# Two of four batches' gates, choices, places and scatters moved from behind the attention into its later pairs

## The chip, the cores and the metric

The kernel runs on one core of a Trainium2 chip. The metric is the device time in microseconds (us) of one execution. Five instruction queues run beside one another and meet only at semaphores: PE (TensorE, matrix products, with PEld for its weight loads), DVE (VectorE), ACT (ScalarE), POOL (GpSimd) and SP (SyncE, which here only issues DMAs).

## The reference

```
x = x + attention(layernorm(x))     # x: 4 batches x 512 tokens x 128; 16 heads of 8, causal, rotary
x = x + ffn(layernorm(x))           # first mixture of experts
x = x + scan_block(layernorm(x))    # convolution, linear recurrence over 512 steps, gate
x = x + ffn(layernorm(x))           # second, same weights

def ffn(x):                         # 2048 tokens, 8 experts, hidden width 512
    scores = sigmoid(x @ Wg.T + bg + bias)
    top_scores, top_idx = top_k(scores, 2)
    # every token: two experts, each gelu(x @ W1[e].T + b1[e]) @ W2[e].T + b2[e], weighted by its score
    # plus one shared expert that every token passes: gelu(x @ Ws1.T + bs1) @ Ws2.T + bs2
```

## The kernel before, in words

**Attention** works through 32 pairs of heads, eight pairs to a batch, so batch b is in pairs 8b to 8b+7. In pair n, PE makes the plain scores of pair n+2 in three units (`scores`, S), DVE takes their row maxima (`row_max`, line 1894, then `split_max`, line 1903), PE makes the turned scores of pair n with the maximum folded in (`scores_T`, T, also three units, line 1360), ACT takes their exponential (`exps`, line 960) and PE weighs the values with them (`weigh_values`, line 1385). Every second pair ACT copies the weighed sums (line 965), PE folds them (line 1397) and DVE divides (lines 1911, 1912). All S and T units, and the few units of the next batch's projections and of the last batch's output projection ("at", "wo"), take turns in three PSUM slots in an order written out by hand (`ring_order`): a unit waits until the unit three turns ahead of it has been read. Lists such as `XN_IN` and `STATS_IN` say behind which pair a side job stands. From pair 17 on ACT and DVE also split the expert weights into high and low halves (lines 1015 and 1953) behind each pair. POOL rotates queries and keys of the next batch (`rope`, lines 766 to 780) and is idle from the end of the last rotation to the end of the attention.

**First feed-forward stage**, behind the attention. For each batch: statistics (`norm_stats`, line 1853), inverse root on POOL (line 729), normalised tokens (`norm_apply`, line 1867), turned on PE (`tokens_T`) and copied by ACT, gate products (`gates`, line 1540) and a sigmoid on ACT, then on DVE `choose` (lines 2059 to 2072: the two best of eight), PE's counts of earlier tokens (`ranks`, line 1552), and `place` (lines 2084 to 2104: the row of each token in its experts' lists). POOL splits the tokens into two halves (`split_rows`) and sends them to those rows in DRAM with eight indirect DMAs a batch (`scatter`, line 879). Some of these wait for named PE units (`BEHIND`), so that they go out spread. Beside this runs the shared expert of each batch: `shared_up` on PE, `shared_hidden` on ACT (lines 1129 and 1140) into one buffer `hid`, `shared_low` on DVE (line 2132), `shared_down` on PE (line 1583), `shared_back` on ACT (line 1149) and `own_outputs` on PE. Since there is one `hid`, a batch's `shared_hidden` waits for the `shared_low` of the batch before it. `map_tiles` (lines 2109 to 2125) turns the filled lists into 39 tiles of 128 rows. PSUM goes round eight banks in a second order written out by hand (`bank_order`). PE fills some waits with products that nobody reads (`stay_awake`, line 1506).

**Tiles**: SP loads each tile's expert weights and rows, PE multiplies (lines 1632, 1646, 1647). SP asks for the first rows when all scatters have landed and the last `shared_low` is done. Then come the scan block, and a second feed-forward stage with the same functions called with r = 1.

The norms are counted: `norm_stats` number n writes `mean[:, n % 8]`, POOL's root of it waits for `var_ready` n+1. In DVE's queue, the order behind the loop of pairs is:

```
for b in range(B - 1): norm_stats(x_all[:, b], core_link, X_SCALE)
for b in range(B - 1): tokens(b)
...
divide(QUADS - 1); tokens_split(0); tokens_split(1); choose(0, 0); attention_post(B - 1); ...
place(0, 0); tokens(3); experts_of(1); experts_of(2); experts_of(3); shared_low(0, 0); ...
```

Of the kernel before, what the change touches and what calls it, by code (L numbers as in the profile page):

```python
# [11 lines left out]
I32 = mybir.dt.int32  # L12
# [33 lines left out]
STATS_IN = {0: 2, 8: 3}  # L46
TOPS_TO = [0, 0, 0, 1, 2, 3, 5, 6, 8, 8, 10, 11, 13, 14] + [16] * (PAIRS - 13)
# [28 lines left out]
EARLY_FILLS = 2 * (PAIRS - FILLS_FROM) - len(SLOTS_IN)  # L76
FFN_LINKS = 7
# [11 lines left out]
def ring_order():  # L89
# [4 lines left out]
    for n in range(PAIRS):  # L94
# [71 lines left out]
def bank_order():  # L166
# [15 lines left out]
    def of_choice(b):  # L182
        return [("gr", 0, b), ("rt", 0, b)]

    order += [("gx", 0, 0), ("gx", 0, 1), ("gg", 0, 0), ("gx", 0, 2), ("gg", 0, 1), ("gg", 0, 2)] + of_choice(0)
    order += of_shared(0, 0) + of_choice(1) + [("gx", 0, 3), ("gg", 0, 3)] + of_choice(2) + of_shared(0, 1) + of_choice(3)
    for b in range(B):
        order += [("sd", 0, b)]
        if b + 2 < B:
            order += of_shared(0, b + 2)  # L190
        order += [("ba", 0, b)]
# [24 lines left out]
RINGS = {"all": (1, 3, 5, 7, 6, 0, 2, 4), "y": (0, 1), "wide": (2, 3, 4), "rest": (5, 6, 7)}  # L216
# [36 lines left out]
def hybrid_block_kernel(nc, x_in, wqkv_in, wo_in, bo_in, w1_in, b1_in, w2_in, b2_in, wg_in, gate_rows_in,  # L253
# [3 lines left out]
    with ExitStack() as ctx:  # L257
# [82 lines left out]
        route = sb("route", [P, TT, X])  # L340
# [55 lines left out]
        ownT = heads_arena[:, 2304:2304 + L]  # L396
        wt = part(arena, 0, [WT, WROW], F16)
# [22 lines left out]
        qk_words = qk_sb[:].rearrange("p t d -> p (t d)")  # L420
        xg = part(qk_words, 0, [XG, ROW], F16)
# [69 lines left out]
        idx_ready = sem("idx_ready")  # L491
        scattered = [sem(f"scattered{b}") for b in range(B)]
        map_ready = sem("map_ready")
        first_in = [sem(f"first_in{e}") for e in range(X)]
# [48 lines left out]
        def x16T_of(r, b):  # L543
            return x16T4[:, b] if r == 0 else x16T[:, b % 2]
# [10 lines left out]
        def xrow_of(r, b):  # L555
            return xrow4[:, b] if r == 0 else xrow[:, b % 2]

        def xrow_words_of(r, b):
            return xrow4_words[:, b] if r == 0 else xrow_words[:, b % 2]
# [32 lines left out]
        def _(sp):  # L592
# [33 lines left out]
            def fill(r, i, start, rows):  # L626
                of = grids[:, FILL_AT + 2 * i:FILL_AT + 2 * i + ROW // 2].bitcast(I32)
                sp.dma_start(rows_dram[r].ap()[start:start + rows, :].rearrange("(n p) d -> p n d", p=P),
                             of.unsqueeze(1).broadcast_to([P, rows // P, ROW // 2])).then_inc(zeroed, 16)
# [96 lines left out]
        def _(pool):  # L726
# [13 lines left out]
            nc.gpsimd.memset(route[:], 1.0)  # L740
# [58 lines left out]
            def take_last(e):  # L799

                pool.wait_ge(first_in[e], 32)
                raw = w1_raw[0:D - 1, e, :]
                nc.gpsimd.tensor_tensor(raw, raw, last_w1[0:D - 1, e * F:(e + 1) * F], ALU.subtract).then_inc(less_last, 1)

# [5 lines left out]
            for e in range(E // 2, E):  # L810
                take_last(e)
            pool.wait_ge(tops_found, 1)
# [3 lines left out]
            rope(3)  # L816

            norms = [B]
# [28 lines left out]
            def set_constants(rows):  # L847

                nc.gpsimd.memset(rows[:, :, :, D - 1], X_SCALE)
                link(nc.gpsimd.memset(rows[:, :, :, 2 * D - 1], 0.0))  # L850

            def split_rows(r, b):

                g = r * B + b
                pool.wait_ge(xf_ready, TT * (g + 1))
                if r == 0:
                    pool.wait_ge(pv_made, PAIRS - 1)
                elif b >= 2:
                    pool.wait_ge(scattered[b - 2], 16 * 2 * TT * 2)
                if g == 0:  # L860
                    set_constants(xrow4)
                high, low = (xrow_of(r, b)[:, :, k * D:(k + 1) * D - 1] for k in range(2))
                tokens = xf_of(r, b)[:, :, 0:D - 1]
                link(nc.gpsimd.tensor_copy(high, tokens))
                nc.gpsimd.tensor_tensor(low, tokens, high, ALU.subtract).then_inc(rows_ready, 1)

            def scatter(r, b):
                g = r * B + b
                pool.wait_ge(idx_ready, g + 1)
                if (r, b) == (1, B - 1):  # L870
                    pool.wait_ge(last_rows_ready, 1)
                else:
# [1547 lines left out]
```

## Time and profile before

| what | value |
|---|---|
| time of three runs | 555.2, 558.01 and 566.67 us, median 558.01 us |
| the profiled execution | 557.48 us, its span from first to last instruction 555.5 us |
| busy share of the span | PE 85%, DVE 77%, ACT 60%, PEld 56%, POOL 49% |
| mean granted TensorE clock | 0.952 of full speed |

The span is what the trace shows; the time of an execution has some us around it. The busy shares are means over very different stages, so the rows that matter are those of the later pairs and of the stage behind them.

### The profile page before, as it was taken

The numbers are of one execution on the slowest core, as the hardware profiler recorded it, in microseconds if no ns is written. First come the engines' busy times: TensorE is split into PE (matmuls) and PEld (weight loads), VectorE is DVE, ScalarE is ACT, GpSimd is POOL, SyncE is SP. The second block draws the span as 40 slices with busy tenths as digits, with TensorE's granted clock in tenths as the row PEclk, the third lists the DMA queues.
The fourth block names the chain that finished last, engine by engine and source line by source line (L and its number), as shares of the span: only waits on it lengthen the run. The fifth ranks groups of instructions, "written<-read, shape, count | busy, mean of one in ns | idle before, by whom it ended". The sixth has DMA issues, their size and how long they took to land.

```text
span 555.5 us, 14159 instructions
## 1 busy us (share of the span) xinstructions
PE 473.2 (85%) x4943; PEld 312.0 (56%) x4943; DVE 426.1 (77%) x1154; ACT 334.7 (60%) x509; POOL 270.8 (49%) x263
## 2 busy tenths in 40 slices
PE   7899988989999968789999898679999995998930
PEld 2436555655665645435579895124455653887930
DVE  5658689778899869777279985798899772888836
ACT  1337556666777773356479984246666861887830
POOL 5418597006400005687328766473275771566650
PEclk9979989999999999979899999979999998999985
DMA  4745796342531463111468691999010014796826
GB/s 130 187 150 169 210 227 156 103 127 81 145 98 32 119 190 106 35 44 49 133 198 260 206 301 54 247 194 170 3 38 20 31 53 126 221 286 197 265 66 200
DMA packets 88186, 78.16 MB, mean 141 GB/s; under 512 B 9917, under 2 KB 72790, under 8 KB 88118
## 3 DMA queue, kind: packets, MB, share of 16 engines
q1 hardware_dynamic: 76208, 57.81, 39.5%
q10 hardware_dynamic: 7366, 10.07, 5.9%
q0 software_dynamic: 4544, 9.38, 4.9%
q8 instruction: 41, 0.67, 0.5%
q14 instruction: 27, 0.22, 0.1%
HBM read 39.92 MB, written 30.88 MB: 127 GB/s over the span
## 4 chain that ended last, share of the span: by engine, by line
PE 31%; DVE 9%; issue 4%; DMA 3%; ACT 2%; SPq 1%; POOL 1%; POOLq 0%; DVEq 0%; ACTq 0%
PE ps L1632 9%; PE ps L1646 6%; PE ps L1647 3%; PE ps L1506 3%; PE ps L1583 2%; DMA arena<-y_dram 2%; PE ps L1622 2%; SPq L712 1%; DVE x_all L2188 1%; PE ps L1718 1%; PE ps L1561 1%; PE ps L1708 1%; DVE arena L2132 1%; DMA y_dram<-arena,goes_to 1%; PE ps L1596 1%
## 5 line engine op out<-in xcount | busy, mean ns | idle before, releaser
L1894 DVE TENSOR_REDUCE max_words<-ps 128x2 f32<-128x256 f32 (+3 forms) x128 | 98.6, 819 | 28.4 <-PE ps L1334 28.2
L888 POOL DMA_INDIRECT y_dram<-arena,goes_to x78 | 86.4, 1108 | 64.7 <-DVE goes_to L2147 35.0
L960 ACT ACTIVATE probs<-ps 128x768 f32<-128x768 f32 (+1 forms) x96 | 80.9, 881 | 31.0 <-PE ps L1365 30.9
L729 POOL TENSOR_TENSOR rstd<-var_eps,minus_half 128x4 f32<-128x4 f32 x16 | 17.5, 1092 | 133.6 <-DVE var_eps L1861 133.6
L879 POOL DMA_INDIRECT rows_dram<-probs,idx x64 | 66.5, 1038 | 23.2 <-issue 18.4
L1632 PE MATMUL ps<-arena 128*128 128x128 f16 x936 | 65.6, 221 | 7.0 <-issue 6.2
L1173 ACT ACTIVATE arena<-ps,up_back 128x512 f32<-128x512 f32 x78 | 53.5, 686 | 25.2 <-PE ps L1632 25.0
L1646 PE MATMUL ps<-w,probs 128*128 x312 | 60.6, 275 | 4.1 <-DVE probs L2159 3.9
L2159 DVE SCALAR_TENSOR_TENSOR probs<-arena,hid_scale,probs 128x512 f16<-128x512 f32 x78 | 58.6, 751 | 6.0 <-ACT probs L1178 3.8
L1506 PE MATMUL ps<-w,ident_f 128*128 128x512 f16 x184 | 51.8, 398 | 11.8 <-issue 4.3
L1632 PEld LDWEIGHTS ps<-arena 128*128 128x128 f16 x936 | 56.0, 98 | 8.4 <-issue 8.3
L1178 ACT ACTIVATE probs<-arena,hid_scale 128x512 f16<-128x512 f32 x78 | 56.3, 722 | 2.6
L1647 PE MATMUL ps<-w,probs 128*128 x312 | 56.2, 221 | 0.0
L1385 PE MATMUL ps<-probs,v_tok 128*32 128x256 f32 (+3 forms) x512 | 42.3, 447 | 4.4 <-ACT probs L960 4.3
L1360 PE MATMUL ps<-heads_arena 64*128 64x512 bf16 (+3 forms) x256 | 37.0, 302 | 9.0 <-ACT probs L960 5.1
L1329 PE MATMUL ps<-heads_arena 62*128 62x128 bf16 (+3 forms) x256 | 36.7, 307 | 5.0 <-DMA heads_arena<-q_words 2.9
L2167 DVE TENSOR_REDUCE arena<-ps 128x128 f32<-128x256 f32 x78 | 32.7, 419 | 9.9 <-PE ps L1647 9.9
L1506 PEld LDWEIGHTS ps<-w,ident_f 128*128 128x128 f16 x184 | 16.8, 102 | 33.8 <-issue 11.3
L1646 PEld LDWEIGHTS ps<-w,probs 128*128 128x128 f16 x312 | 30.6, 98 | 8.4 <-issue 5.5
L1334 PE MATMUL ps<-mask_qk,neg_eye 64*128 64x128 bf16 x512 | 34.7, 219 | 0.0
L1129 ACT ACTIVATE arena<-ps,b,up_back 128x512 f32<-128x512 f32 x32 | 23.1, 771 | 14.2 <-DVE arena L2132 7.6
L1385 PEld LDWEIGHTS ps<-probs,v_tok 128*32 128x32 f32 x512 | 20.9, 111 | 18.9 <-issue 9.9
(234 smaller groups left out, 1011.1 us busy)
## 6 DMA issues: line engine op xcount, KB each, us to landing
arena<-weights_dram SPq DMA_DIRECT2D x78, 256.0 KB
rows_dram<-grids SPq DMA_DIRECT2D x64, 260.0 KB, 4.2
heads_arena<-q_words SPq DMA_DIRECT2D x45, 128.0 KB, 2.5
qk_sb<-rows_dram SPq DMA_DIRECT2D x78, 65.0 KB
arena<-in_w ACTq DMA_DIRECT2D x3, 768.0 KB, 9.1
arena<-in_w ACTq DMA_DIRECT2D x9, 256.0 KB, 3.3
weights_dram<-w SPq DMA_DIRECT2D x2, 1152.0 KB, 8.1
w<-in_last_w ACTq DMA_DIRECT2D x8, 256.0 KB, 3.9
```

What stands on the lines that cost most here:

```text
L879: nc.gpsimd.indirect_dma_start(rows_dram[r].ap(), bass.IndirectOffsetOnAxis(ap=idx[:, r, b, t, k:k + 1], axis=0), xrow_words_of(r, b)[:, t ...
L888: nc.gpsimd.indirect_dma_start(y_dram.ap(), bass.IndirectOffsetOnAxis(ap=goes_to[:, n % AT_GO:n % AT_GO + 1], axis=0), y_t[:, n % YT, :], ...
L960: nc.scalar.activation(probs[:, n % 2, :, PROB_AT[u]:PROB_AT[u] + size], ps[:, of:of + 2, 0:size], ACT.Exp).then_inc(slot_free[slot_of(("T ...
L1173: nc.scalar.activation(hid_t[:, n % HT, :], ps[:, of, :], ACT.Gelu, scale=up_back[:]).then_inc(bank_free[of], 1)
L1178: nc.scalar.activation(hid16_t[:, n % HT, 0, :], hid_t[:, n % HT, :], ACT.Identity, scale=hid_scale[:]).then_inc(high_t_ready, 1)
L1385: mm = pe.matmul(ps[group:group + OW, PV_BANK, j * P:L], v_flat[:, at_v:at_v + OW], probs[:, n % 2, h, at[j]:at[j] + L - P * j], start=(p ...
L1506: pe.matmul(ps[:, to, :], ident_f16[:], w1[:, 0, 0, :], start=True, stop=True, skip_group_check=True)
L1632: mm = pe.matmul(ps[:, to, c * P:(c + 1) * P], w1t[:, s % WT, w, c * P:(c + 1) * P], xgT[:, n % GT, v, :], start=((w, v) == (0, 0)), stop= ...
L1646: pe.matmul(halves, hid16_t[:, n % HT, 0, c * P:(c + 1) * P], parts, start=(c == 0), stop=False, skip_group_check=True)
L1647: mm = pe.matmul(halves[:, 0, :], hid16_t[:, n % HT, 1, c * P:(c + 1) * P], parts[:, 0, :], start=False, stop=(c == C - 1), skip_group_che ...
L1894: ins = nc.vector.tensor_reduce(max_words[:, n % 2, :, t], ps[:, of:of + 2, o:o + keys], AX.X, ALU.max)
L2159: nc.vector.scalar_tensor_tensor(hid16_t[:, n % HT, 1, :], hid_t[:, n % HT, :], hid_scale[:], hid16_t[:, n % HT, 0, :], ALU.mult, ALU.subt ...
```

## The change

Batches 0 and 1 (`EARLY = 2`) get their statistics, gates, choices, places and scatters behind pairs 11 to 25; batch 2's statistics move behind pair 28. The early gate takes the exponential that attention already uses, and DVE finishes the sigmoid with an addition and a reciprocal. Early units take turns in the three slots. Their buffers lie in memory of the rotation tables and of the last rotation's work. The chosen scores get one buffer a batch (`route_all`). The DRAM fills are sent in another order, so that the parts which early scatters write are filled first, and counted apart. Three expert-weight loads share one semaphore. Behind the attention the bank order, PE's, ACT's, DVE's and POOL's orders of the first stage are new, `BEHIND` is empty for it, and several `stay_awake` calls go.

```diff
+EARLY = 2
+GATE_STATS_IN = {11: 0, 19: 1, 28: 2}
+GATE_APPLY_IN = {12: 0, 21: 1}
+GATE_TURN_IN = {13: 0, 22: 1}
+GATES_IN = {14: 0, 23: 1}
+CHOICE_IN = {15: 0, 24: 1}
+RANKS_IN = {16: 0, 25: 1}
...
-        for name, steps in (("xn", XN_IN), ("q", Q_IN), ("k", K_IN), ("v", V_IN)):
+        for name, steps in (("xn", XN_IN), ("q", Q_IN), ("k", K_IN), ("v", V_IN), ("early", GATE_TURN_IN),
+                            ("scores", GATES_IN), ("ranks", RANKS_IN)):
...
+    (0, 0): {},
+    (0, 1): {},
+    (0, 2): {},
+    (0, 3): {},
...
-            fills += [(r, i, i * B * L + j * FILL_ROWS * P, FILL_ROWS * P) for i in range(E) for j in range(B * L // (FILL_ROWS * P))]
+            fills += [(r, i, i * B * L + j * FILL_ROWS * P, FILL_ROWS * P) for j in range(B * L // (FILL_ROWS * P)) for i in range(E)]
```

On POOL:

```diff
+            def early_root(b):
+                n = B + b
+                inverse_root(n)
+                pool.wait_ge(rstd_ready, n + 1)
+                nc.gpsimd.tensor_tensor(shift[:, n % NORMS], mean[:, n % NORMS], rstd[:, n % NORMS], ALU.mult).then_inc(far_shift, 1)
+            def early_split(b):
+                pool.wait_ge(slot_free[slot_of(("early", b))], filled(("early", b)))
+                high, low = (early_x16T[:, b, v, :] for v in range(2))
+                link(nc.gpsimd.tensor_copy(high, early_xnT[:, b, :]))
+                nc.gpsimd.tensor_tensor(low, early_xnT[:, b, :], high, ALU.subtract).then_inc(early_x16_ready, 1)
...
+            early_root(0)
+            split_rows(0, 0)
             pool.wait_ge(tops_found, 1)
...
             rope(3)
+            early_split(0)
+            pool.wait_ge(early_filled, 16 * EARLY * E)
+            scatter(0, 0, range(0, 2))
+            early_root(1)
+            scatter(0, 0, range(2, TT))
+            pool.wait_ge(placed, 16 * len(PLACINGS) * B)
+            split_rows(0, 1)
+            early_split(1)
+            scatter(0, 1)
```

On ACT, in the pairs and behind them:

```diff
+            def early_apply(b):
+                n = B + b
+                act.wait_ge(far_shift, B + b)
...
+                for t in range(TT):
+                    nc.scalar.activation(early_xf[:, t, :], x_all[:, b, t, :], ACT.Identity, bias=shift[:, n % NORMS, t:t + 1],
+                                         scale=rstd[:, n % NORMS, t:t + 1]).then_inc(early_xf_ready, 1)
+            def early_tokens(b):
+                of = take(("early", b))
+                nc.scalar.copy(early_xnT[:, b, :], ps[:, of, :]).then_inc(slot_free[slot_of(("early", b))], 1)
+            def early_scores(b):
+                of = take(("scores", b))
+                nc.scalar.activation(score[:, b, :, 0:E], ps[:, of, 0:TT * E].rearrange("p (t e) -> p t e", t=TT),
+                                     ACT.Exp, scale=-1.0 / X_SCALE).then_inc(slot_free[slot_of(("scores", b))], 1)
...
+            tokens_T(2)
+            gates(0, 2)
             post_tokens(B - 1)
             route_T(0, 0)
             route_T(0, 1)
+            shared_hidden(0, 0)
             tokens_T(3)
             gates(0, 3)
+            shared_hidden(0, 1)
+            shared_back(0, 0)
             route_T(0, 2)
+            shared_hidden(0, 2)
+            shared_back(0, 1)
             route_T(0, 3)
+            shared_hidden(0, 3)
+            shared_back(0, 2)
+            shared_back(0, 3)
```

On PE:

```diff
+            def early_tokens(b):
+                to = give(("early", b))
+                for t in range(TT):
+                    pe.wait_ge(early_xf_ready, b * TT + t + 1)
+                    mm = pe.transpose(ps[:, to, t * P:(t + 1) * P], early_xf[:, t, :], ident[:])
+                mm.then_inc(slot_full[slot_of(("early", b))], 1)
+            def early_products(b):
+                read_by(("early", b))
+                pe.wait_ge(ffn_in, 16 * len(ffn_loads))
+                pe.wait_ge(scale_rows_ready, 1)
+                to = give(("scores", b))
...
+                for t in range(TT):
+                    mm = pe.matmul(gates[:, t * E:(t + 1) * E], early_xnT[:, b, t * P:(t + 1) * P], wg[:], start=False,
+                                   stop=True, skip_group_check=True)
+                mm.then_inc(slot_full[slot_of(("scores", b))], 1)
+            def early_counts(b):
+                to = give(("ranks", b))
+                pe.wait_ge(sel_ready, b + 1)
...
+                for k in range(TT):
+                    mm = pe.matmul(places[:, (k + 1) * E:(TT + 1) * E], counts[:, 1, :], flat[:, 0:(TT - k) * E],
+                                   start=False, stop=(k == TT - 1), skip_group_check=True)
+                mm.then_inc(slot_full[slot_of(("ranks", b))], 1)
...
+            tokens_T(0, 2)
             weighed_T(QUADS - 1)
+            gates(0, 2)
+            route_T(0, 0)
             post_tokens(B - 1)
+            route_T(0, 1)
+            project(B - 1)
+            ranks(0, 2)
...
             shared_up(0, 0)
+            shared_up(0, 1)
             tokens_T(0, 3)
             gates(0, 3)
+            shared_down(0, 0)
+            ranks(0, 3)
+            route_T(0, 2)
+            own_outputs(0, 0)
+            shared_up(0, 2)
+            shared_down(0, 1)
+            route_T(0, 3)
+            own_outputs(0, 1)
+            shared_up(0, 3)
```

On DVE:

```diff
+            def early_gate(b):
+                dve.wait_ge(slot_free[slot_of(("scores", b))], filled(("scores", b)))
+                of = score[:, b, :, 0:E]
+                post_link(nc.vector.tensor_scalar(of, of, 1.0, None, ALU.add))
+                post_link(nc.vector.reciprocal(of, of))
...
+                if n in GATE_STATS_IN:
+                    norm_stats(x_all[:, GATE_STATS_IN[n]], pre_link, X_SCALE, minus=GATE_STATS_IN[n] < EARLY)
+                if n in CHOICE_IN:
+                    early_gate(CHOICE_IN[n])
+                    choose(0, CHOICE_IN[n])
+                if n in RANKS_IN:
+                    place(0, RANKS_IN[n])
...
-            for b in range(B - 1):
-                norm_stats(x_all[:, b], core_link, X_SCALE)
-            for b in range(B - 1):
-                tokens(b)
+            tokens(2)
...
             divide(QUADS - 1)
-            tokens_split(0)
-            tokens_split(1)
-            choose(0, 0)
+            choose(0, 2)
             attention_post(B - 1)
...
-            place(0, 0)
+            place(0, 2)
             tokens(3)
-            experts_of(1)
-            experts_of(2)
-            experts_of(3)
+            tokens_split(2)
             shared_low(0, 0)
-            tokens_split(2)
+            choose(0, 3)
+            place(0, 3)
+            map_tiles(0)
             tokens_split(3)
             shared_low(0, 1)
             shared_add(0, 0)
-            map_tiles(0)
```

## Rows read from the trace of the kernel before

**Rows 1.** Chain that ended last, at the first stage's end: start us, us, what.
```profile
268.21 0.68 ACT heads_arena L1149
...
271.11 3.91 PE ps L1583 x12
...
280.26 0.84 PE ps L1632 x12
```
**Rows 2.** Timeline of PE, DVE, ACT behind the attention; brackets: idle before, releaser.
```profile
207.94 1.28 PE L1385 MATMUL ps<-probs,v_tok 128*32 128x512 f32 x16 [1.86 <-ACT probs L960]
...
209.77 5.89 DVE L1867 TENSOR_SCALAR heads_arena<-x_all,mean,rstd 128x128 f32<-128x128 f32 x12
...
221.68 0.69 DVE L1919 TENSOR_TENSOR x_all<-ps,x_all 128x512 f32<-128x512 f32 x1 [0.77 <-PE ps L1412]
...
234.98 1.45 ACT L1129 ACTIVATE arena<-ps,b,up_back 128x512 f32<-128x512 f32 x2
...
247.57 1.45 ACT L1129 ACTIVATE arena<-ps,b,up_back 128x512 f32<-128x512 f32 x2 [3.47 <-DVE arena L2132]
...
263.16 1.45 ACT L1129 ACTIVATE arena<-ps,b,up_back 128x512 f32<-128x512 f32 x2 [3.32 <-DVE arena L2132]
...
264.01 2.75 PE L1583 MATMUL ps<-arena,w 128*128 128x512 f16 x12
```
**Rows 3.** Scatters, by tile: duration ns min/median/max, first and last start.
```profile
L879 POOL DMA_INDIRECT rows_dram<-probs,idx x32: 955/967/1605, 225.9 to 269.6; - x32
```
**Rows 4.** Timeline of DVE in the same stage.
```profile
219.16 0.40 DVE L2059 MAX8 best<-score 128x8 f32<-128x16 f32 x4
...
220.72 0.19 DVE L2072 TENSOR_TENSOR route<-score,sel 128x32 f32<-128x32 f32 x1
...
222.40 0.87 DVE L1853 BATCH_NORM_STATS2 stats<-x_all 128x6 f32<-128x128 f32 x4
...
224.01 0.17 DVE L2084 COPY filled_rows<-grids 128x8 f32<-128x8 f32 x1
...
226.50 1.11 DVE L1867 TENSOR_SCALAR heads_arena<-x_all,mean,rstd 128x128 f32<-128x128 f32 x4
...
256.29 0.17 DVE L2109 TENSOR_TENSOR n_of<-filled_rows,grids 128x8 f32<-128x8 f32 x1
...
260.58 2.49 DVE L2132 SCALAR_TENSOR_TENSOR arena<-arena,hid_scale 128x1024 f16<-128x1024 f32 x2
```
**Rows 5.** Windows over later pairs: us; busy of PE, PEld, DVE, ACT, POOL; clock, DMA.
```profile
100.00:140.00 40.00, 36.80 (x529) 23.53 (x529) 30.82 (x61) 25.15 (x38) 10.33 (x10) 1.00 0.39 106
140.00:180.00 40.00, 37.17 (x587) 24.48 (x583) 36.44 (x61) 30.72 (x49) 5.36 (x5) 1.00 0.36 95
```
**Rows 6.** Timeline of DVE and PE in two later pairs.
```profile
159.66 1.88 DVE L1894 TENSOR_REDUCE max_words<-ps 128x2 f32<-128x256 f32 x3
...
161.60 0.34 PE L1360 MATMUL ps<-heads_arena 64*128 64x384 bf16 x2
...
189.82 3.02 DVE L1894 TENSOR_REDUCE max_words<-ps 128x2 f32<-128x256 f32 x4
...
191.76 0.34 PE L1360 MATMUL ps<-heads_arena 64*128 64x384 bf16 x2 [0.36 <-DVE max_words L1894]
```
**Rows 7.** Timeline of ACT in two pairs, and PE's gate products behind the attention.
```profile
95.51 0.88 ACT L976 ACTIVATE xn<-x_all,shift,rstd 128x128 f32<-128x128 f32 x2
...
161.07 0.59 ACT L965 COPY weighed<-ps 128x512 f32<-128x512 f32 x1
...
232.37 1.06 PE L1540 MATMUL ps<-wg,heads_arena 128*128 128x8 f32 x8
```
**Rows 8.** Timeline of POOL and DVE: `split_max` beside the last rotation, and alone.
```profile
137.32 1.27 POOL L770 TENSOR_TENSOR rope_c<-rope_c,rope_s 128x512 f32<-128x512 f32 x1
...
138.02 0.60 DVE L1903 TENSOR_TENSOR max_words<-max_words 128x8 bf16<-128x8 f32 x1
...
198.19 0.17 DVE L1903 TENSOR_TENSOR max_words<-max_words 128x8 bf16<-128x8 f32 x1
```

More of the change, by code:

```diff
@@ L211 @@
 AT = {unit: i for i, unit in enumerate(bank_order())}
-RINGS = {"all": (1, 3, 5, 7, 6, 0, 2, 4), "y": (0, 1), "wide": (2, 3, 4), "rest": (5, 6, 7)}
+AT_SLOT, WO_SLOT = (TURN[(name, B - 1)] % RING for name in ("at", "wo"))
+REST_SLOT = 3 - AT_SLOT - WO_SLOT
+FIRST_BANKS = (2 * AT_SLOT + 1, 2 * WO_SLOT + 1, 2 * REST_SLOT, 2 * REST_SLOT + 1)
+RINGS = {"all": FIRST_BANKS + (6, 7, 2 * AT_SLOT, 2 * WO_SLOT), "y": (0, 1), "wide": (2, 3, 4), "rest": (5, 6, 7)}
 def ring_of(unit):
@@ new lines, in split_rows @@
+            def split_rows(r, b):
+                g = r * B + b
+                if g < EARLY:
+                    pool.wait_ge(early_xf_ready, TT * (g + 1))
+                    set_constants(early_rows[b])
+                else:
+                    pool.wait_ge(xf_ready, xf_count(r, b, TT))
+                    if r == 0:
+                        pool.wait_ge(pv_made, PAIRS - 1)
+                    elif b >= 2:
+                        pool.wait_ge(scattered[b - 2], 16 * 2 * TT * 2)
+                    if g == EARLY:
+                        set_constants(xrow4[:, EARLY:B])
+                high, low = (xrow_of(r, b)[:, :, k * D:(k + 1) * D - 1] for k in range(2))
+                tokens = (early_xf if g < EARLY else xf_of(r, b))[:, :, 0:D - 1]
+                link(nc.gpsimd.tensor_copy(high, tokens))
+                nc.gpsimd.tensor_tensor(low, tokens, high, ALU.subtract).then_inc(rows_ready, 1)
@@ new lines, in scatter @@
+            def scatter(r, b, of_t=range(TT)):
+                g = r * B + b
+                pool.wait_ge(idx_ready, g + 1)
+                if (r, b) == (1, B - 1):
+                    pool.wait_ge(last_rows_ready, 1)
+                else:
+                    pool.wait_ge(rows_ready, g + 1)
+                for t in of_t:
+                    for k in range(2):
+                        unit = BEHIND[r, b].get(2 * t + k)
+                        if unit is not None:
+                            pool.wait_ge(bank_full[bank_of(unit)], count_of(unit))
+                        nc.gpsimd.indirect_dma_start(rows_dram[r].ap(), bass.IndirectOffsetOnAxis(ap=idx[:, r, b, t, k:k + 1], axis=0),
+                                                     xrow_words_of(r, b)[:, t, :].bitcast(I32), None).then_inc(scattered[b], 16)
@@ L845, in residual @@
                 nc.gpsimd.tensor_tensor(x_all[:, b], x_all[:, b], xsf[:, b], ALU.add).then_inc(residual_ready, 1)
[L847 to L872, printed above, removed]
-                    pool.wait_ge(rows_ready, g + 1)
-                for t in range(TT):
-                    for k in range(2):
-                        unit = BEHIND[r, b].get(2 * t + k)
-                        if unit is not None:
-                            pool.wait_ge(bank_full[bank_of(unit)], count_of(unit))
-                        nc.gpsimd.indirect_dma_start(rows_dram[r].ap(), bass.IndirectOffsetOnAxis(ap=idx[:, r, b, t, k:k + 1], axis=0),
-                                                     xrow_words_of(r, b)[:, t, :].bitcast(I32), None).then_inc(scattered[b], 16)
             def tiles(r):
@@ L2037, in _ @@
                     scan_weights()
-            for b in range(B - 1):
-                norm_stats(x_all[:, b], core_link, X_SCALE)
-            for b in range(B - 1):
-                tokens(b)
+            tokens(2)
             def tokens_split(b):
```

262 lines of the change are left out of this document (139 added, 123 removed), and 4 rows, old and new, of the table BEHIND.

## The prediction

> **What bounds the kernel now.** I read the chain of waits first, where the change works: the end of the first feed-forward stage. There the chain goes ACT's `shared_back`, PE's `shared_down` and on to the first tile product at 280.26 us [rows 1]. So the shared expert's chain sets the start of the tiles. The timeline behind the attention says why it is late: the last values are weighed at 207.94 + 1.28 = 209.22 us, which I call T, but the first `shared_hidden` starts at 234.98 (T + 25.8), the second at 247.57 after 3.47 us of waiting for DVE, the fourth at 263.16 after 3.32 us for DVE [rows 2]. From the fourth's start to `shared_back` is 268.21 - 263.16 = 5.05 us, from there to the first tile 12.05 [rows 1, 2]. POOL's scatters are a second chain almost as long: 32 of them from 225.9 to 269.6, (269.6 - 225.9) / 31 = 1.41 us apart [rows 3]. The stage lasts 280.26 - 209.22 = 71.0 us.
>
> The place to which the work goes is not empty. In the later pairs PE is busy 36.8 and 37.2 of 40 us, DVE 30.8 and then 36.4 [rows 5]. The slots couple the two: PE's second unit of turned scores starts 161.60 - 159.66 = 1.94 us after DVE begins its row maxima, and again 191.76 - 189.82 = 1.94 where DVE came late and PE idled 0.36 for it [rows 6]. A delay of DVE behind a pair thus reaches PE nearly whole.
>
> **Cost in the attention.** DVE's pieces, from the same work behind the attention: statistics 224.01 - 222.40 = 1.6 us, choice 220.72 + 0.19 - 219.16 = 1.75, place 226.50 - 224.01 = 2.5 [rows 4]. The addition and reciprocal of the early gate are of the size of the choice's last small piece, 0.19 [rows 4]; with the link between them I estimate 0.5. Three statistics, two gates with choice, two places: 4.8 + 4.5 + 5.0 = 14.3 us.
> - The one behind pair 11 falls into the window where DVE idles 9.2 of 40 us [rows 5]; I count 0.5 of its 1.6.
> - Behind pairs 16, 24 and 28 an odd pair follows, without the folded sums, where PE catches up about what it idled, 0.36 [rows 6]: -1.1.
> - Behind pair 25 the counts come after the "at" unit. DVE waits for them as it does for PE's projection, 0.77 [rows 2]: +0.7.
> That makes 14.3 - 1.1 - 1.1 + 0.7 = 12.8 us on the path.
>
> PE's gate products, 1.06 us a batch [rows 7], stand alone behind pairs 14 and 23: 2 us. The turns and counts stand where DVE is late anyway: nothing; without that cover, about 1 us a batch, of the size of the gate products. ACT's `early_apply` is twice a row of two that takes 0.88, so about 1.65 [rows 7]. Behind pair 12 ACT waits for PE afterwards; I count 0.5. Behind pair 21 the next copy of weighed sums (161.07) follows other ACT work with no idle time noted [rows 7], so exponentials and PE's folding queue behind the 1.65; DVE's second weight piece there covers some: 1.0. Early copies and the exponential of 32 numbers go into ACT's idle time, 9.3 of 40 us [rows 5].
>
> POOL gets two roots, two row splits, two token splits and 16 scatters before the attention ends. Its busy time hides itself: 5.4 of 40 us [rows 5]. But DVE's `split_max` took 0.60 us beside a rotation and 0.17 alone [rows 8]. The scatters alone are 16 x 1.41 = 23 us [rows 3], the rest about another 10: some seven pairs of 4.7 us (191.76 - 161.60 = 30.2 us is between 6 and 7 of them) [rows 6]. If half their `split_max` meets POOL: 7 x 0.43 / 2 = 1.5. Between zero and 7 x 0.43 = 3, I take 1. Waits of POOL's queue (early fills, last placings) hold up only its own early work: batch 1's place stands behind pair 25, six pairs or 28 us before the end, and its scatters need 8 x 1.41 = 11. On SP only the order of fills is new; it and the joined load semaphores cost nothing, since the fills that early scatters need are sent first and POOL has idle time before its next late user (were that gone, the rotation of batch 3 would come late, with the slack of two pairs).
>
> Stretch: 12.8 + 2 + 1.5 + 1 = 17.3. Some of these delays fall in the same pair and then count once (the gate products of pair 23 and the choice of pair 24, ACT and the two weight pieces at 21 and 22): -2. **The attention gets 15.5 us longer**, with ends 8 (half of it packs into DVE's and PE's idle time) and 22 (all of 14.3, everything of PE and ACT, 3 of POOL).
>
> **Gain behind it**, in us after T. DVE's twelve applies, 5.89 us ahead of the last division, are gone (batch 2's four fit before T) [rows 2], so the last residual addition moves from 221.68 - 209.22 = 12.5 to 6.6. The inputs of `shared_up` of batch 0 then lie ready, and the first hidden starts after a quarter of 2.75 us of products [rows 2], near 7.7 instead of 25.8. The second needs `shared_low` of batch 0, which on DVE stands behind addition 0.7, statistics 1.6, place 2.5, tokens 1.1 [rows 4] and a token split (about as long as the tokens): 6.6 + 7.0 = 13.6, and 2.5 for itself [rows 4] gives 16.1. Batch 3's sigmoid stands between the two on ACT; I take 16.8. The third needs `shared_low` of batch 1, now behind choice 1.75, counts that wait for PE's `shared_down` (2.75 [rows 2], until about 19.4), place 2.3, `map_tiles` with one small product 260.58 - 256.29 = 4.3 [rows 4], a split 1.1: 27.1, and 29.6 when done. It runs 5.05 to 34.6. The fourth waits for `shared_back`, `own_outputs` and only then `shared_up` of batch 3, which stands behind them on PE: 34.6 + 0.7 [rows 1] + some 1.1, as the gate's small products [rows 7], + 0.7 = 37.1, to 42.2. Add 12.05 [rows 1]: first tile at T + 54.2. **The stage loses 71.0 - 54.2 = 16.8 us.** Only 16 scatters remain behind the attention, done by about 10 + 16 x 1.41 + 2 = 35: no longer a bound. Ends: 12, if PE's products between run like `shared_down` at 3.91 instead of 2.75 us [rows 1, 2] in four places, since the dummy products are fewer; 21, if the third hidden is not late by its 4.3 of `map_tiles`.
>
> **Sum.** 15.5 - 16.8 = -1.3. The profiled execution took 557.48 us (2 outside its span); 556.2 after it. The median lies 0.5 above that execution, so about 556 to 557; I say 556.
>
> **Rivals.**
> *The pairs absorb the work.* DVE idles 9.2 and 3.6 us in the two windows, PE 3.2 and 2.8 [rows 5]. If the idle time closes up, the stretch is 8 or less and the time 557.5 + 8 - 18 = 547, or 544 with less. For it: no engine is full. Against: PE waited as soon as DVE was late [rows 6].
>
> *POOL and DVE get in each other's way (slower).* Every two-input DVE operation among the pairs then waits for a POOL operation. About 20 such (`split_max` and low weights, ten pairs) and 25 of statistics, choices and places would stand beside POOL. The rows show 0.43 more for one [rows 8], with a whole POOL operation of 1.27 us [rows 8] the worst. 45 x 0.43 = 19 us instead of my 1: 557.5 - 1.3 + 18 = 574. It decides from 0.28 us each on (45 x 0.28 = 12.5, where slower by 2% begins). Against it: two thirds of POOL's early time are scatters, which read a list of rows and not whole tiles as the rotation does. The Trainium skill, SBUF — State Buffer, section "Who interferes with whom", says that DVE and GpSimd share one port pair as an exclusive lock, so that the loser waits for a whole instruction; the trace agrees for the rotation (0.60 against 0.17), and by that rule the sum would be this rival's.
>
> *The stage does not shorten.* The single `hid` buffer keeps hidden, low, hidden in a row, and the third waits as reckoned. If the second is as late too, the stage loses 12 or less: 557.5 + 15.5 - 11 = 562.
>
> **How the numbers follow.** Chances: forecast 0.54 (549 to 562), absorbed 0.24 (540 to 549), stage not shortened 0.12 (560 to 567), port 0.10 (566 to 576). Two per cent, about what a measurement of this kernel can tell from no change, is 546.8 and 569.2. Faster: most of the absorbed case, 0.2; slower: the port case but for its lower end, 0.09; within 0.71. The range leaves a tenth out on each side: 545 to 567; the forecast's own is 549 to 562.
>
> **What would show it.** Right: the last line-1385 group near 225 us instead of 209; row maxima behind pairs 15, 16, 24, 25 late by two us with PE idle "DVE max_words"; first Gelu some 8 us after T; fourth hidden about T + 37; first tile near 279; from there on all as before. Wrong: T below 218; `split_max` over 0.5 us in most pairs of 18 to 28; first tile later than T + 60; or scatters still running then.

## The result and the profile after

The changed kernel takes 567.63 us (median of 16 runs, 560.4 to 574.26), the kernel before beside it 559.42 (16 runs, 553.11 to 567.19). The ratio is 1.0159, 95% interval 1.012 to 1.0198: 1.6% slower, where I had forecast 556 us, no change. The time lies just outside the range of 545 to 567. This ratio and those below compare only the executions of each kernel that are not long ones, within some 1.5% of its shortest, so 1.0159 is not the quotient of the two medians.

| profiled execution, us | before | after | change | forecast |
|---|---|---|---|---|
| span | 555.5 | 564.4 | +8.9 | -1.3 |
| first scores of the pair before the added work | 94.86 | 92.39 | -2.5 | 0 |
| T, end of the attention | 209.22 | 229.61 | +20.4 | +15.5 |
| T to first `shared_hidden` | 25.8 | 9.5 | -16.2 | -18.1 |
| T to fourth `shared_hidden` | 53.9 | 42.1 | -11.8 | -16.8 |
| T to first tile product | 71.0 | 59.3 | -11.7 | -16.8 |
| first tile to the end of the span | 275.2 | 275.5 | +0.2 | 0 |

The span is that of the one profiled execution of each kernel. Counted from the table's second row, the attention got 20.4 + 2.5 = 22.9 us longer. The timeline of the changed kernel behind the attention answers to [rows 1, 2] (start us, us, engine, line, operation, idle before and releaser):

```profile
228.33 1.28 PE L1462 MATMUL ps<-probs,v_tok 128*32 128x512 f32 x16 [1.86 <-ACT probs L1014]
...
237.34 0.69 DVE L2030 TENSOR_TENSOR x_all<-ps,x_all 128x512 f32<-128x512 f32 x1 [2.07 <-PE ps L1489]
...
239.14 1.45 ACT L1207 ACTIVATE arena<-ps,b,up_back 128x512 f32<-128x512 f32 x2 [1.60 <-PE ps L1680]
...
248.33 1.45 ACT L1207 ACTIVATE arena<-ps,b,up_back 128x512 f32<-128x512 f32 x2
...
254.96 0.17 DVE L2248 TENSOR_TENSOR n_of<-filled_rows,grids 128x8 f32<-128x8 f32 x1
...
259.97 2.48 DVE L2271 SCALAR_TENSOR_TENSOR arena<-arena,hid_scale 128x1024 f16<-128x1024 f32 x2
...
262.54 1.45 ACT L1207 ACTIVATE arena<-ps,b,up_back 128x512 f32<-128x512 f32 x2 [8.04 <-DVE arena L2271]
...
271.71 0.78 ACT L1207 ACTIVATE arena<-ps,b,up_back 128x512 f32<-128x512 f32 x1 [2.99 <-PE ps L1680]
```

The last residual addition comes at T + 7.7 (before T + 12.5), the first Gelu follows. But the third hidden layer waits 8.04 us for DVE's low halves of batch 1 (line 2271), which start only at 259.97, behind `place(0, 3)`, `map_tiles` (254.96 to 258.9) and a token split. The scatters, the second chain of before [rows 3], leave POOL at 264.94 + 0.97 = 265.9, 23 us ahead of the first tile. The chain that ended last runs through the fourth hidden layer:

```profile
267.59 0.68 ACT heads_arena L1227
...
268.31 2.08 PE ps L1713 x8
270.39 4.64 PE ps L1680 x12
...
275.68 2.59 PE ps L1700 x12
...
288.92 0.84 PE ps L1749 x12
```

Lines 1713 and 1680 (`own_outputs` and `shared_up`) take 2.08 and 4.64 us here. The windows say why (us; busy us of PE, its loads, DVE, ACT, POOL; granted clock, DMA share, GB/s): between 230 and 275 us the granted clock is 0.85 on the mean (before 0.89). It is 0.85 already among the pairs from 130 us on, where it was 1.00 before.

```profile
94.00:130.00 36.00, 33.04 (x460) 21.04 (x450) 28.85 (x74) 23.56 (x39) 3.73 (x8) 1.00 0.39 104
130.00:165.00 35.00, 26.45 (x352) 17.74 (x345) 29.32 (x68) 17.59 (x27) 24.81 (x23) 0.85 0.35 94
230.00:275.00 45.00, 37.85 (x193) 22.71 (x192) 27.77 (x102) 28.51 (x38) 19.98 (x19) 0.85 0.18 54
```

In the kernel before, the window among the pairs reads:

```profile
130.00:165.00 35.00, 32.85 (x513) 22.41 (x509) 29.98 (x50) 26.37 (x43) 15.13 (x13) 1.00 0.42 113
```

In that window PE is busy 26.45 us after the change and 32.85 before. There lies the largest single loss. The time between two first products of plain scores (62x128, line 1406; 1329 before) tells what a pair takes; I call it the pair's period. Two neighbours stand out: 4.62 and 6.02 us before, 7.83 and 12.64 after. They hold the choice and the place of batch 0. The timelines of POOL and of DVE at the place:

```profile
135.14 1.27 POOL L795 TENSOR_TENSOR rope_c<-q_words,k_words 128x512 f32<-128x512 f32 x1
136.36 1.27 POOL L796 TENSOR_TENSOR rope_s<-q_words,k_words 128x512 f32<-128x512 f32 x1
137.71 1.28 POOL L798 TENSOR_TENSOR rope_c<-rope_c,rope_s 128x512 f32<-128x512 f32 x1
138.94 1.26 POOL L799 TENSOR_TENSOR rope_c<-rope_c,rope_s 128x512 f32<-128x512 f32 x1
```

```profile
135.62 0.81 DVE L2146 COPY filled_rows<-grids 128x8 f32<-128x8 f32 x1
136.47 0.19 DVE L2153 TENSOR_TENSOR rows_of<-ps,filled_rows 128x32 f32<-128x32 f32 x1
...
136.78 0.90 DVE L2157 TENSOR_TENSOR rows_of<-rows_of,sel 128x32 f32<-128x32 f32 x1
137.71 0.19 DVE L2158 TENSOR_REDUCE two_rows<-rows_of 128x4 f32<-128x32 f32 x1
...
138.03 0.98 DVE L2160 TENSOR_TENSOR two_rows<-row_sum,two_rows 128x4 f32<-128x4 f32 x1
139.04 1.20 DVE L2165 COPY k_words<-two_rows 128x4 f32<-128x4 f32 x1
...
140.54 0.94 DVE L2170 TENSOR_TENSOR of_row<-of_row,route 128x64 f32<-128x64 f32 x1
...
141.77 0.89 DVE L2173 TENSOR_SCALAR wts<-wts_raw,down_back 128x8 f32<-128x8 f32 x1
142.69 3.17 DVE L2005 TENSOR_REDUCE max_words<-ps 128x2 f32<-128x256 f32 x4
```

The place lasts 142.69 - 135.62 = 7.07 us; [rows 4] had 2.5 for the same work. Six operations took 0.81 to 1.20 us, together 5.72. Their ends lie at ends of POOL's: 135.62 + 0.81 = 136.43 at 136.41, 138.03 + 0.98 = 139.01 at 138.99, 139.04 + 1.20 = 140.24 at 140.20. The reduction and the addition that reads `ps` took their 0.19 while a POOL operation ran. PE stood still meanwhile, 4.50 us, which answers to the 0.36 of [rows 6]:

```profile
143.78 0.61 PE L1406 MATMUL ps<-heads_arena 62*128 62x512 bf16 x2 [4.50 <-DVE max_words L2005]
```

### The profile page after: what moved, and what is told of

Read it like the earlier page. It is cut to its first block, busy times and chain, and to the rows that moved or that the text cites. A ratio compares the mean times of both kernels' runs of the same rounds, so it can differ in the third digit from the quotient of the medians.

```text
span 564.4 us, 14120 instructions
## 1 busy us (share of the span) xinstructions
PE 471.4 (84%) x4913; PEld 313.9 (56%) x4913; DVE 425.6 (75%) x1146; ACT 340.7 (60%) x519; POOL 277.2 (49%) x273
## 4 chain that ended last, share of the span: by engine, by line
PE 33%; DVE 9%; issue 4%; DMA 3%; ACT 2%; SPq 1%; POOL 1%; POOLq 0%; DVEq 0%; ACTq 0%
PE ps L1749 9%; PE ps L1763 6%; PE ps L1764 3%; PE ps L1620 3%; PE ps L1700 3%; DMA arena<-y_dram 2%; PE ps L1680 2%; PE ps L1739 1%; PE ps L1713 1%; DVE x_all L2327 1%; DVE x_all L2323 1%; PE ps L1835 1%; DVE arena L2271 1%; PE ps L1825 1%; DMA y_dram<-arena,goes_to 1%
## 5 line engine op out<-in xcount | busy, mean ns | idle before, releaser
L945 POOL DMA_INDIRECT y_dram<-arena,goes_to x78 | 87.9, 1128 | 74.5 <-DVE goes_to L2286 49.1
L1251 ACT ACTIVATE arena<-ps,up_back 128x512 f32<-128x512 f32 x78 | 53.5, 686 | 23.2 <-PE ps L1749 22.9
L871 POOL DMA_INDIRECT rows_dram<-probs,idx x48 | 50.1, 1044 | 20.8 <-issue 14.4
L1406 PE MATMUL ps<-heads_arena 62*128 62x128 bf16 (+3 forms) x256 | 36.6, 306 | 16.2 <-DVE max_words L2005 12.7
L1620 PE MATMUL ps<-w,ident_f 128*128 128x512 f16 x154 | 42.2, 392 | 9.2 <-issue 4.0
L1462 PE MATMUL ps<-probs,v_tok 128*32 128x384 f32 (+3 forms) x512 | 42.6, 449 | 4.1 <-ACT probs L1014 4.1
L1442 PE MATMUL ps<-mask_kq,neg_eye 64*128 64x128 bf16 x512 | 32.3, 220 | 0.0
```

The costliest lines, as they stand in the source:

```text
L871: nc.gpsimd.indirect_dma_start(rows_dram[r].ap(), bass.IndirectOffsetOnAxis(ap=idx[:, r, b, t, k:k + 1], axis=0), xrow_words_of(r, b)[:, t ...
L945: nc.gpsimd.indirect_dma_start(y_dram.ap(), bass.IndirectOffsetOnAxis(ap=goes_to[:, n % AT_GO:n % AT_GO + 1], axis=0), y_t[:, n % YT, :], ...
L1251: nc.scalar.activation(hid_t[:, n % HT, :], ps[:, of, :], ACT.Gelu, scale=up_back[:]).then_inc(bank_free[of], 1)
L1462: mm = pe.matmul(ps[group:group + OW, PV_BANK, j * P:L], v_flat[:, at_v:at_v + OW], probs[:, n % 2, h, at[j]:at[j] + L - P * j], start=(p ...
L1620: pe.matmul(ps[:, to, :], ident_f16[:], w1[:, 0, 0, :], start=True, stop=True, skip_group_check=True)
```

## The experiments

Theory: two steps failed, separate from each other. The place of batch 0 stands beside POOL's rotation of batch 3 (132.7 to 147.2 us), whose operations hold up DVE's (I call that the port), and the third hidden layer of the stage waits for low halves that DVE's order puts behind `map_tiles`. Rivals: a place is dear wherever it stands; the missing `stay_awake` products made the stage slow through the clock. Ratios are to the kernel before, run on the same chips.

**The price of the port alone.** The kernel before, with eight small operations of DVE behind pair 16 (beside the rotation) and again behind pair 20 (POOL idle):

```diff
+            def probe():
+                post_link(nc.vector.memset(rows_of[:], 1.0))
+                post_link(nc.vector.tensor_copy(filled_rows[:], rows_of[:, 0]))
+                post_link(nc.vector.tensor_tensor(rows_of[:], rows_of[:], rows_of[:], ALU.mult))
+                post_link(nc.vector.tensor_reduce(row_sum[:], rows_of[:], AX.X, ALU.add))
+                post_link(nc.vector.tensor_tensor(row_sum[:], row_sum[:], row_sum[:], ALU.subtract))
+                post_link(nc.vector.tensor_copy(two_rows[:, :, 0], row_sum[:]))
+                post_link(nc.vector.tensor_scalar(rows_of[:], rows_of[:], 1.0, None, ALU.mult))
+                post_link(nc.vector.tensor_tensor(rows_of[:], rows_of[:], filled_rows[:].unsqueeze(1).broadcast_to([P, TT, E]), ALU.add))
...
+                if n in (16, 20):
+                    probe()
```

> The kernel before with eight small operations of DVE put behind pair 16, where POOL rotates batch 3, and the same eight behind pair 20, where POOL is idle (a fill, a copy, a product, a reduction, a difference, a copy, a scaled copy, a sum with a broadcast operand; 128x4 to 128x32; they write scratch that is written again before it is read). Port theory: behind pair 20 each takes 0.16 to 0.2 us, 1.6 together; behind pair 16 the copies, the scaled copy and the two-input operations without a broadcast take 0.5 to 1.3 each, the fill, the reduction and the broadcast sum stay near 0.2, 5 to 7 us together. Rival (it is the places' own waits on PE and on links that made it long): both 1.6 to 2.

Ratio 1.0105 (1.0051 to 1.0158), of two executions only. The timeline of DVE in that kernel, beside the rotation and behind pair 20:

```profile
132.51 0.09 DVE L1985 MEMSET rows_of<- 128x32 f32 x1
132.63 0.67 DVE L1986 COPY filled_rows<-rows_of 128x8 f32<-128x8 f32 x1
133.33 1.22 DVE L1987 TENSOR_TENSOR rows_of<-rows_of 128x32 f32<-128x32 f32 x1
134.59 0.19 DVE L1988 TENSOR_REDUCE row_sum<-rows_of 128x4 f32<-128x32 f32 x1
134.81 1.05 DVE L1989 TENSOR_TENSOR row_sum<-row_sum 128x4 f32<-128x4 f32 x1
135.90 1.19 DVE L1990 COPY two_rows<-row_sum 128x4 f32<-128x4 f32 x1
137.12 0.18 DVE L1991 TENSOR_SCALAR rows_of<-rows_of 128x32 f32<-128x32 f32 x1
137.34 0.91 DVE L1992 TENSOR_TENSOR rows_of<-rows_of,filled_rows 128x32 f32<-128x32 f32 x1
...
158.96 0.09 DVE L1985 MEMSET rows_of<- 128x32 f32 x1
159.08 0.17 DVE L1986 COPY filled_rows<-rows_of 128x8 f32<-128x8 f32 x1
159.29 0.19 DVE L1987 TENSOR_TENSOR rows_of<-rows_of 128x32 f32<-128x32 f32 x1
159.51 0.18 DVE L1988 TENSOR_REDUCE row_sum<-rows_of 128x4 f32<-128x32 f32 x1
159.73 0.16 DVE L1989 TENSOR_TENSOR row_sum<-row_sum 128x4 f32<-128x4 f32 x1
159.93 0.17 DVE L1990 COPY two_rows<-row_sum 128x4 f32<-128x4 f32 x1
...
160.35 0.19 DVE L1992 TENSOR_TENSOR rows_of<-rows_of,filled_rows 128x32 f32<-128x32 f32 x1
```

From the fill to the last sum it is 137.34 + 0.91 - 132.51 = 5.74 us beside the rotation and 160.35 + 0.19 - 158.96 = 1.58 alone. The pair's period grows by 5.89 (6.02 to 11.91) and by 1.23 (4.54 to 5.77). The operations are the same and so is the kernel; what differs is POOL. So the price does not come from the place's own waits, the rival of this run. I was wrong on two of them: the sum with a broadcast operand took 0.91, and the scaled copy 0.18. The latter began at 137.12, in the gap between POOL operations that ended at 137.06 and began at 137.13, so it says nothing against the others; the scaled copy of the changed kernel (line 2173) took 0.89.

**The place moved behind pair 20.**

```diff
-RANKS_IN = {16: 0, 25: 1}
+RANKS_IN = {20: 0, 25: 1}
...
-            scatter(0, 0, range(0, 2))
             early_root(1)
-            scatter(0, 0, range(2, TT))
+            scatter(0, 0)
```

> Batch 0's counts and place move from behind pair 16, beside POOL's rotation of batch 3, to behind pair 20, where POOL runs no whole-tile work (its root for batch 1 moves ahead of the scatters so that ACT does not wait). Theory port: the place took 7.07 us instead of 2.49 because its two-input operations queued behind POOL's; here it takes 2.5 +- 0.3, pairs 16 and 17 shrink by 4.5 us or more, ratio to the kernel before 1.005 to 1.010 (from 1.016). Rival slots: the added PSUM units and the waits around them make the pair long; then the place's length and the loss only move to pair 20 and the ratio stays 1.014 to 1.018.

Ratio 1.0071 (1.0031 to 1.0111), 0.9% below the changed kernel, as expected. Alone, no operation of the place takes over 0.23 us (timeline of DVE):

```profile
160.95 0.16 DVE L2145 COPY filled_rows<-grids 128x8 f32<-128x8 f32 x1
...
161.94 0.18 DVE L2156 TENSOR_TENSOR rows_of<-rows_of,sel 128x32 f32<-128x32 f32 x1
...
163.65 0.23 DVE L2172 TENSOR_SCALAR wts<-wts_raw,down_back 128x8 f32<-128x8 f32 x1
```

Of the long six, the same lines take 1.13 us here instead of 5.72: the 4.6 by which the place was too long. The two periods take 7.54 + 6.66 = 14.2 us instead of 20.5. But the pairs behind it pay more, so that in these two profiles the whole stretch is only 0.6 us shorter, as the rival had it. The stage is 56.8 us long instead of 59.3. By these rows, then, the place is short here, but the gain of 0.9% in time isn't located.

**The place behind pair 18, alone** (`RANKS_IN = {18: 0, 25: 1}`, nothing else).

> The changed kernel with the place of batch 0 behind pair 18 and nothing else. Theory (the two causes add up: the change 1.016, the order of the low halves -0.014, both together 0.991): the stretch of the attention 134 us instead of 137, the stage 56 to 59 us as in the changed kernel, ratio to the kernel before 1.003 to 1.008, 562 to 564 us. Rival (the 0.991 is one chip's or one series' luck): ratio as with the place behind pair 20 or above, 1.007 to 1.012.

Ratio 1.0075 (1.0039 to 1.0111). The stretch of the attention is 133.0 us; three profiles of the unmoved place (this change, and two kernels below with the same attention) give 137.2, 139.8 and 139.2, the kernel before 114.4. The stage takes 57.8 us, and the third hidden layer again waits 8.02 us for the low halves. Ratio, stretch and stage are as expected. The place's period grows by 3.5 us (8.03, before 4.51) instead of 6.6. POOL's row split of batch 0 (147.3 to 149.2 us) still meets two operations of the place (0.40 and 0.93 us).

**POOL's rotation of batch 3 held back until the place has written its rows.**

```diff
             pool.wait_ge(scales_ready, 1)
+            pool.wait_ge(idx_ready, 1)
             add_bias(3)
```

> The place stays behind pair 16; POOL's rotation of batch 3 waits until the place has written its row numbers. Theory port: the same gain from the other side, place 2.5 to 3 us (its tail still meets the first rotation product), pairs 16 and 17 shorter by 3.5 to 4.5 us, ratio 1.006 to 1.012; some split_max operations of pairs 18 to 20 turn slow instead. Rival slots: no change, 1.014 to 1.018. A second rival: the rotation comes late for pair 22's scores, then PE shows a wait for the placed heads and the ratio rises above 1.018.

Ratio 1.0045 (1.0003 to 1.0086), 1.1% below the changed kernel and better than I expected. Up to 142.48, where POOL's work for batch 3 now starts, the place's operations take 0.16 to 0.22 us; then the product takes 1.33, the reduction 0.22 and the scaled copy 0.89. The span of this profile, 567.1 us, lies above the median of the runs, so I draw nothing from its other rows, and where the 1.1% arose isn't shown.

**DVE's order in the stage.** The low halves of batch 1 ahead of `map_tiles`:

```diff
             place(0, 3)
-            map_tiles(0)
-            tokens_split(3)
             shared_low(0, 1)
+            tokens_split(3)
+            map_tiles(0)
             shared_add(0, 0)
```

> Behind the attention DVE does the second shared_low right after the place of batch 3, ahead of the token split and of the map of tiles. Theory chain: the third shared_hidden waits for that operation alone, so it starts 4.5 to 5 us earlier after the end of the attention (from T + 32.9 to about T + 28) and the first tile comes 3 to 5 us earlier, ratio 1.007 to 1.011. Rival: PE's own products and the lower clock set the chain from there on; then the third hidden is earlier but the first tile by under 1.5 us, ratio 1.013 to 1.018.

Ratio 1.0021 (0.9977 to 1.0066), 1.4% below the changed kernel and better than expected. The third hidden layer starts at T + 26.7, the first tile at T + 52.3 instead of T + 59.3, although the attention here is no shorter (139.8 us, T at 232.79).

**Both together**, run on two occasions:

> The place of batch 0 stands behind pair 18 instead of 16 (POOL's rotation is over by then), and DVE's low halves of batch 1 go ahead of map_tiles. Theory (the two causes are separate and add up): place about 2.5 to 3 us long, the two periods between first turned scores that took 20.5 us take 14 to 15, the third hidden starts T + 26 to 28, the first tile T + 52 to 54; against the changed kernel 3.5 + 6 us less, so about 558 us where the kernel before has 559.5, ratio 0.994 to 1.003. Rival (what is gained in the attention is given back in the pairs that take the place, as with pair 20): attention no shorter, ratio 1.002 to 1.007.

> The first kernel of the second series (place behind pair 18, low halves of batch 1 ahead of map_tiles) once more, beside the kernel before on another occasion. If its gain holds: ratio 0.987 to 0.997, first tile 50 to 53 us after the end of the attention. If it was luck: 0.998 to 1.002, as its two relatives gave.

Ratios 0.9907 (0.9862 to 0.9951) and 0.9944 (0.991 to 0.9979), 555.48 and 555.97 us: 0.6 to 0.9% faster than the kernel before, and within their intervals the two gains add up (1.0159 - 0.0084 for the place - 0.0138 for the order = 0.994). The first of the two came out better than expected. The stages are 50.7 and 50.6 us long. The timeline of ACT and DVE of the second:

```profile
250.36 2.48 DVE L2271 SCALAR_TENSOR_TENSOR arena<-arena,hid_scale 128x1024 f16<-128x1024 f32 x2
...
252.94 1.45 ACT L1207 ACTIVATE arena<-ps,b,up_back 128x512 f32<-128x512 f32 x2 [3.02 <-DVE arena L2271]
...
261.38 1.45 ACT L1207 ACTIVATE arena<-ps,b,up_back 128x512 f32<-128x512 f32 x2 [2.27 <-DVE arena L2271]
```

The low halves start at T + 24.1 (226.24 + 24.1) instead of T + 30.4, and the wait of 8.04 us is 3.02. The window behind the attention shows what came with it, without a dummy product restored:

```profile
230.00:275.00 45.00, 40.65 (x244) 24.18 (x242) 31.07 (x105) 30.27 (x41) 20.87 (x19) 1.00 0.19 57
```

The clock is 1.00 where the changed kernel has 0.85; the profile of the first occasion has 1.00 too, the moved place alone 0.85, the new order alone 0.92. Beside the moved place alone, the new order shortens the stage by 57.8 - 50.6 = 7.2 us. Of these, 5.0 are there at the start of the third hidden layer (T + 31.7 against T + 26.7), where the wait shrank by 8.02 - 3.02 us; up to the second, both profiles agree. Only the other 2.2 us, behind it, can have come through the clock.

**More of the same.** The low halves ahead of `place(0, 3)` too, and POOL's split of batch 3's rows ahead of the scatters of batch 2:

```diff
             choose(0, 3)
+            shared_low(0, 1)
             place(0, 3)
-            shared_low(0, 1)
...
+            split_rows(0, 3)
             scatter(0, 2)
-            split_rows(0, 3)
             scatter(0, 3)
```

> As the run before it, and in addition DVE's low halves of batch 1 go ahead of place(0, 3) too, and POOL splits the rows of batch 3 ahead of the scatters of batch 2, so that place(0, 3) doesn't run beside that split. Theory (the third hidden's start is set by the low halves of batch 1): third hidden near T + 24 instead of T + 26.7, place(0, 3) 2.5 us instead of 4.06, first tile near T + 50, 2 us less than the run before it. Rival (the fourth hidden hangs on PE's products at their lower clock, or the tiles on map_tiles): first tile stays at T + 52 and the time that of the run before it within 1 us.

Ratio 0.9985 (0.9949 to 1.0021). `place(0, 3)` takes 2.3 us instead of 4.1, but the third hidden layer stays at T + 26.8, now after 2.27 us of waiting for PE's `shared_up`, and the first tile at T + 51.9. The rival was right on the wait: the low halves no longer end it. But the median, 558.0, is 2.5 us above that of the kernel with both edits on the same occasion, more than I had allowed, and the stage explains only 1.2 of it.

**The dummy products.** The `stay_awake` calls restored in the changed kernel (in `tokens_T`, `ranks` and `route_T`), with 8 and 12 products that the kernel before did not have ahead of the first two `own_outputs`, and the same in the kernel with both edits:

```diff
-                if r * B + b > EARLY:
-                    stay_awake(to, 3)
+                stay_awake(to, 3)
...
+                if r == 0:
+                    stay_awake(to, 2)
...
+                if r == 0 and b < EARLY:
+                    stay_awake(to, (8, 12)[b])
```

> The dummy products that the change took out of the first stage are back (3 ahead of the turned tokens and the counts, 2 ahead of the turned scores), and 8 and 12 more stand ahead of the first two own outputs, where PE idled. Theory clock: granted clock in the stage rises, project and turned scores run at their full-speed durations (project 1.1 instead of 1.8 us, shared_up of batch 3 2.7 instead of 4.9), first tile 2 to 4 us earlier after T, ratio 1.009 to 1.013. Rival: the dummies stand on the path themselves and cost what they give, ratio 1.014 to 1.019.

> As the first of this call, with the removed stay_awake products restored. Clock theory: the stage's granted clock is 1.00 instead of some 0.9 and the first tile comes 2 to 3 us earlier, near T + 50: 0.4 to 0.5% below the first run of this call. Rival (the dummy products cost PE what the clock gives back, now that PE and not DVE ends the waits): no difference within 0.2%.

In the changed kernel: ratio 1.0147 (1.0087 to 1.0208), from six executions, not told apart from 1.0159; the 1.009 to 1.013 of the clock theory is not confirmed. The window of its stage has the clock at 1.00:

```profile
230.00:275.00 45.00, 41.81 (x252) 24.08 (x253) 28.45 (x103) 29.59 (x40) 20.62 (x22) 1.00 0.17 51
```

The stage is 55.9 us long there, 3.4 shorter, but the third hidden layer still waits 8.04 us for DVE. With both edits the dummies give 0.9992 (0.9954 to 1.003), a stage of 53.3: no gain, rather a loss against 0.9907 and 0.9944, where the clock theory had a gain of 0.4 to 0.5%. So the clock's part in the stage is up to 3.4 us by one profile, and less beside three others without the dummies, where the stage takes 56.8, 57.8 and 57.8 us; the times don't show it.

## Why the prediction was wrong

**The direction of each step was right**: the first Gelu soon after T, row maxima late with PE waiting for "DVE max_words", the fourth hidden as the stage's end, scatters no longer a bound, all later work as before. The gain and the cost are both there. What failed are sizes, from -1.3 to the profile's +8.7 at the first tile: 22.9 us in the attention, beyond even its end of 22, and a gain of 11.7 in the stage, at its end of 12.

**The place of batch 0: 7.07 us instead of 2.5.** I took [rows 4] from a stretch in which POOL ran no operation on whole tiles, only an inverse root on 128x4 (224.26 to 225.27) and a scatter, beside which the place's operations took 0.16 to 0.23. I put the port's price at 1 us for the whole attention, counting `split_max` alone; [rows 8] has the rotation and its 0.60. I named the rival and spread it over 45 operations at 0.43 us. In fact six operations in one place bear it, some 0.76 more each (4.6 / 6), and the rest almost none: beside the scatters `split_max` took 0.17 to 0.20 us. So the argument against the rival (scatters are not rotations) held for 16 scatters, and missed that `RANKS_IN` 16 and the rotation released by `set_scales` behind pair 15 meet. The timeline of POOL before showed it, the rotation from 131.06 to 145.5 with pair 16 in the middle:

```profile
131.06 1.27 POOL L766 TENSOR_TENSOR rope_c<-q_words,k_words 128x512 f32<-128x512 f32 x1
...
144.34 1.16 POOL L780 TENSOR_TENSOR q_words<-rope_s,q_words 128x512 bf16<-128x512 f32 x1
```

The timeline of scatters beside DVE in the changed kernel (POOL, then DVE):

```profile
200.56 0.96 POOL L871 DMA_INDIRECT rows_dram<-q_words,idx  x1 [0.30 <-issue]
201.82 0.95 POOL L871 DMA_INDIRECT rows_dram<-q_words,idx  x1 [0.30 <-issue]
```

```profile
201.23 0.17 DVE L2014 TENSOR_TENSOR max_words<-max_words 128x8 bf16<-128x8 f32 x1
```

The Trainium skill, SBUF — State Buffer, section "Who interferes with whom", adds what I had read past: copies and `tensor_scalar` can take the shared pair too, a reduction never does, and the loser is blocked for the whole of the other's instruction. The traces agree on all three: 1.19 for a copy and 0.89 for a scaled copy, 0.19 for the reduction, and ends that fall together with POOL's.

**The other terms of the attention** were short by 22.9 - 15.5 - 4.6 = 2.8 us. The periods, after less before, tell where (a job of DVE behind pair n delays the period that begins with the first scores of pair n + 3). The statistics behind pair 19 cost 1.6 us (reckoned 1.6), the place behind pair 25 2.2 (reckoned 3.2), the statistics behind pair 28 1.1 (reckoned 1.6 - 0.36). But the choice behind pair 15 cost 3.2 where I had 2.25, and the jobs behind pairs 21 to 24 together 6.4, where I had 3.9 and had even taken 2 off for delays in the same pair. A slip besides: 17.3 - 2 is 15.3, not 15.5.

**The stage: 11.7 us less instead of 16.8.** Its end to the first tile was right (17.2 us against 5.05 + 12.05 = 17.1). The misses add up ahead of it: first hidden 1.8 late (1.1 of it the residual addition, at T + 7.7 behind PE's transposes and projection of 1.06 and 1.81 us, which took 0.64 and 1.14 before; the rest the addition's own 0.69, which the sum left out), third 3.3 late (of which 1.8 is `place(0, 3)` at 4.06 us, beside POOL's row split), fourth 5.0 late (`own_outputs` and `shared_up` 2.08 and 4.64 us, where 1.16 and 2.75 are at full clock). So two terms were too small here: PE's products at the lower clock, some 1.1 + 1.7 us of the 5.0, a slowness that I had named as the reason for the end of 12 and left out of the middle; and `place(0, 3)` beside POOL, 1.8. I had also put `map_tiles` and a split, 4.3 + 1.1 us, in front of the low halves in the sum and taken that order as given; turning it round took 7 us away, 5.0 of them from the wait itself.

**"The pairs absorb the work"** is refuted: no profile of the changed attention is below 133 us against 114.4. **"The stage does not shorten"** had the size of the stage's gain right (12 or less, measured 11.7) but by another way, a second hidden layer as late as the third; the second came at T + 18.7 (forecast T + 16.8), no later against the forecast than the first.

Open stays the 2.5 us by which the profile of after was ahead at 92.39: nine other profiles of kernels with the change have 92.25 to 94.75, two without the change 93.40 and 94.86, so it may be scatter.

## What to carry to other kernels

A duration taken from one stretch holds in another only if the neighbours are the same: before moving small VectorE work, lay it against GpSimd's timeline at the new place, and count an overlapped copy or two-input operation at up to one whole GpSimd instruction where that works on whole tiles (0.8 to 1.3 us here). When a move gains less than it should, look at which wait ends last in the place where the gain was due; here a change of order on one engine was worth about as much as the costliest mistake (0.0138 and 0.0084 of the ratio, with overlapping intervals), and dummy products for the clock, once that wait was shorter, bought nothing.

## What was not expected of the hardware

A 128x4 copy of 0.17 us takes up to 1.20 us beside a GpSimd operation on 128x512, seven times as long, and the eight probe operations 5.74 against 1.58 us. GpSimd's indirect DMA instructions of about 0.96 us, almost as long, showed no such effect on `split_max`, nor did its inverse root on 128x4 (1.01 us) on the place's operations in [rows 4]. With the stalls TensorE's clock fell as well. In the changed kernel the granted clock is 0.60 on the mean from 134.7 to 138.7 us, after PE had idled 1.70 us for the row maxima behind the choice, and 0.53 from 143.7 to 148.4 us, after the 4.50 us beside the place. Between 130 and 165 us it is 0.85, where the kernel before has 1.00 and the one with the probe 0.95. The first product of scores behind the 4.50 us took 0.61 us, where the same one took 0.39 at 132.37.
